# Feed-forward of a fused two-layer network on one core: 704 hidden units in six tiles of 128 rows instead of eight of 88, and 28 TensorE products without a reader

## The reference, cut to what matters

```python
def _act_fake_quant(x, clip_factor):
    scale = jax.nn.sigmoid(clip_factor) * jnp.max(jnp.abs(x)) / QMAX
    return jnp.clip(_ste_round(x / scale), -QMAX - 1.0, QMAX) * scale
...
xq = _act_fake_quant(x, clip_x[0])                                      # x: (16, 113, 256)
gate = jnp.einsum('bsh,ih->bsi', xq, _weight_fake_quant(w_gate))        # i = 704 units
up = jnp.einsum('bsh,ih->bsi', xq, _weight_fake_quant(w_up))
h = _act_fake_quant(jax.nn.silu(gate) * up, clip_down[0])
return jnp.einsum('bsi,hi->bsh', h, _weight_fake_quant(w_down))
```

## Time and profile before

| | |
|---|---|
| median of 3 runs | 865.48 us (865.08 to 865.71) |
| the profiled execution | 865.44 us, of which the span of its instructions 863.5 us |
| PE busy over the span | 699.7 us (81%) |
| DVE, ACT, POOL busy | 520.7, 392.2, 351.2 us |
| mean granted clock of TensorE | 0.89 of full speed |
| end of the state-space stage, start of the feed-forward | about 776 us |
| first and last start of a gate or up product (L1620) | 791.7, 819.8 us |
| first and last start of a down product (L1634) | 832.0, 859.1 us |

### The profile page before, as it was taken

How to read it: one execution, slowest core, us unless ns; L and a number is a source line. 1 busy time by engine, 2 the same in 40 slices (tenths; PEclk the granted TensorE clock), 3 DMA queues, 4 the chain that set the end, 5 groups by cost and what they waited for, 6 DMA issues and landing times. The chain is left out here.

```text
span 863.5 us, 12104 instructions
## 1 busy us (share of the span) xinstructions
PE 699.7 (81%) x3696; PEld 474.2 (55%) x3697; DVE 520.7 (60%) x931; ACT 392.2 (45%) x858; POOL 351.2 (41%) x332
## 2 busy tenths in 40 slices
PE   7699999997999957999994788897788785535958
PEld 5577777775655524665663555455456452213557
DVE  1555555555231102544436568988988988974974
ACT  0465555554422103233222456665665662106973
POOL 0021111110035802323221158878878888420625
PEclk9899999997999968999997789999999997566955
DMA  9990000000002153111114202201210220000002
GB/s 274 335 416 20 0 0 0 0 2 0 1 7 39 31 104 114 44 49 43 43 36 98 88 1 87 87 29 59 86 54 34 87 87 0 0 0 1 0 11 76
DMA packets 28696, 52.73 MB, mean 61 GB/s; under 512 B 10965, under 2 KB 23545, under 8 KB 26489
## 3 DMA queue, kind: packets, MB, share of 16 engines
q1 hardware_dynamic: 19929, 47.49, 16.6%
q0 software_dynamic: 8736, 4.85, 2.2%
HBM read 42.62 MB, written 9.60 MB: 60 GB/s over the span
## 5 line engine op out<-in xcount | busy, mean ns | idle before, releaser
L480 POOL TENSOR_TENSOR arena<-arena 128x904 f32<-128x904 f32 x64 | 124.8, 1953 | 59.3 <-DVE arena L1244 53.0
L1244 DVE TENSOR_TENSOR_SCAN arena<-ps,arena 128x452 f32<-128x452 f32 x128 | 133.5, 1085 | 6.7 <-ACT ps L768 2.1
L768 ACT ACTIVATE ps<-arena,sh_w 128x448 f32<-128x448 f32 x128 | 80.3, 635 | 107.7 <-DVE arena L1244 106.9
L1704 PE MATMUL ps<-arena,const 128*128 128x452 f32 x112 | 63.2, 650 | 41.3 <-POOL arena L484 41.3
L554 ACT ACTIVATE work<-ps,work 113x113 f32<-113x113 f32 x256 | 67.1, 420 | 56.3 <-DVE work L899 56.3
L1528 PE MATMUL ps<-arena,work 128*128 x176 | 86.5, 618 | 0.3 <-issue 0.3
L428 POOL TENSOR_TENSOR xT<-work 128x452 f32<-128x452 f32 x16 | 15.1, 943 | 157.7 <-DVE work L888 157.7
L1234 DVE TENSOR_TENSOR arena<-arena,ps 128x904 f32<-128x904 f32 x64 | 69.2, 1082 | 11.1 <-PE ps L1691 10.7
L511 POOL DMA_INDIRECT slots_in<-xn,slot x16 | 37.9, 2366 | 74.1 <-issue 74.1
L484 POOL TENSOR_TENSOR arena<-arena 128x452 f32<-128x452 f32 x56 | 64.1, 1144 | 4.4
L527 POOL DMA_INDIRECT answers_e<-work,slot_token x22 | 23.7, 1076 | 101.5 <-DVE work L1033 101.5
(11 more groups left out here) (239 smaller groups left out, 1428.5 us busy)
## 6 DMA issues: line engine op xcount, KB each, us to landing
arena<-c_rows SPq DMA_DIRECT2D x8, 1808.0 KB, 6.5
arena<-in_ex_w SPq DMA_DIRECT2D x8, 1536.0 KB, 23.6
slots_in<-work SPq DMA_DIRECT2D x1, 2827.0 KB, 22.3
work<-slots_in SPq DMA_DIRECT2D x22, 128.5 KB, 2.1
xn<-answers_e SPq DMA_DIRECT2D x4, 448.0 KB
out<-resid SPq DMA_DIRECT2D x8, 224.0 KB
arena<-in_patches SPq DMA_DIRECT2D x3, 576.0 KB, 6.0
sh_w<-in_sh_w SPq DMA_DIRECT2D x1, 1536.0 KB, 11.4
```

What stands on the lines that cost most here:

```text
L480: pool.tensor_tensor(read[kp], state[kp], c_all[par][:, 2 * c:2 * c + 2, :].unsqueeze(2).broadcast_to([P, 2, KT, N]), ALU.mult)\
L768: act.activation(decay_ps(n)[:, :, 1:], delta[par].rearrange("p k (b s) -> p (k b) s", b=GB)[:, :, 1:], ACT.Exp, scale=a_neg[:, 2 * c + n: ...
L1244: dve.tensor_tensor_scan(state[kp][:, n].rearrange("p k s -> p (k s)"), decay_ps(n).rearrange("p q s -> p (q s)"), drive[kp][:, n].rearran ...
L1704: pe.matmul(ps[:, 6, 0:KT * N], ident, read[kp][:, 0].rearrange("p k s -> p (k s)"), start=False, stop=False, skip_group_check=True).then_ ...
```

## The change

`FT, FP` becomes 6, 128: five full tiles and one of 64 real units. For the weights of gate and up the last tile is filled by repeating unit 703, so `hid` has 64 rows of copies in it, which don't change a maximum; the down projection uses only the first 64 rows of the last tile (`FLAST`). All operations over a tile now have 128 partitions, the rounding of a piece has 6 x 226 elements per partition instead of 8 x 226. The weight tiles in the expert stage go from 16 to 12, and the four steps that no longer carry one are written out. Gate and up are no longer in loops on any engine: 24 tiles are written out one after the other, with the same order of work. And `keep_busy` on TensorE makes products of 452 columns into a bank that nobody reads again: 12 as soon as VectorE's last product is done, 4 behind the spread of the scale, 12 ahead of the down projection.

```diff
-FFN, FT, FP = 704, 8, 88
+FFN, FT, FP = 704, 6, 128
+FLAST = FFN - (FT - 1) * FP
...
         def pe_ffn(pe):
+            def keep_busy(products):
+                for _ in range(products):
+                    pe.matmul(ps[:, 4, 0:4 * S], identb[:, :], xqT[:, 0, 0:4 * S], start=True, stop=True)
+
...
-            with pe.Fori(0, FG) as g:
-                for m in range(FT):
-                    pair = m % 4
-
-                    pe.wait_ge((hid_even, fup_ready)[m % 2], g * (FT // 2) + m // 2 + 1)
...
+            for i in range(FG * FT):
+                g, m, pair = i // FT, i % FT, i % 4
+
+                pe.wait_ge((hid_even, fup_ready)[i % 2], i // 2 + 1)
...
+            pe.wait_ge(fgate_ready, FG * FT)
+            pe.wait_ge(hid_even, FG * FT // 2 + 2)
+            keep_busy(12)
             scales(1, FP)
+            keep_busy(4)
 
             pe.wait_ge(dscale_ready, KT)
             for k in range(KT):
                 last = pe.matmul(ps[:, 6, k * P:(k + 1) * P], onesf[:, :], diag_d[:, k, :], start=True, stop=True, skip_group_check=True)
             last.then_inc(dscaleT_ps, 1)
+            keep_busy(12)
             for b in range(B):
...
                 for m in range(FT):
-                    last = pe.matmul(ps[0:S, b % 4, 0:D], hq[:, m, b * S:(b + 1) * S], dq[:, m, :], start=m == 0, stop=m == FT - 1)
+                    rows = slice(0, FP if m < FT - 1 else FLAST)
+                    last = pe.matmul(ps[0:S, b % 4, 0:D], hq[rows, m, b * S:(b + 1) * S], dq[rows, m, :], start=m == 0, stop=m == FT - 1)
...
-            for n in range(4):
+            for n in range(FT // 2):
                 act.wait_ge(wqT_ps, 2 * FT + n + 1)
-                act.activation(dq[:, 2 * n:2 * n + 2, :], ps[0:FP, 1 + n, :].rearrange("p (m d) -> p m d", m=2), ACT.Copy).then_inc(wqT_ready, 1)
+                for m in range(2 * n, 2 * n + 2):
+                    rows = slice(0, FP if m < FT - 1 else FLAST)
+                    last = act.activation(dq[rows, m, :], ps[rows, 1 + n, m % 2 * D:(m % 2 + 1) * D], ACT.Copy)
+                last.then_inc(wqT_ready, 1)
...
-            with act.Fori(0, FG // 2) as turn:
-                for m2 in range(2 * FT):
...
+            for i in range(FG * FT):
+                m, pair = i % FT, i % 4
...
-            with dve.Fori(0, FG - 1) as g:
-                products_and_maxima(g)
-            products_and_maxima(FG - 1, last=True)
+            for i in range(0, FG * FT, 2):
+                if i + 4 < FG * FT:
+                    product(i + 4)
+                greatest(i)
+                greatest(i + 1)
```

More of the change, by code:

```diff
@@ L181, in build @@
         sh_w = sb("sh_w", [P, EW])
-        xn2_named = sb("xn2", [S, B, D + 1])
+        xn2_all = sb("xn2", [P, B, D + 1])
+        xn2_named = xn2_all[0:S]
         xn2 = xn2_named[:, :, 0:D]
@@ L218, in build @@
         e_y = [pl.take((D,)) for _ in range(2)]
-        w_int = [pl.take((D // 2,), 88).bitcast(BF16) for _ in range(2)]
+        w_int = [pl.take((D // 2,), FP).bitcast(BF16) for _ in range(2)]
         slot_token = sb("slot_token", [P, ETILES], I32)
@@ L445, in pool_ffn @@
             pool.sem_inc(hid_odd, 2)
[L446 to L450, removed]
+            for i in range(1, FG * FT, 2):
+                g, m = i // FT, i % FT
+                pool.wait_ge(fgate_ready, i + 1)
+                pool.wait_ge(fup_ready, i // 2 + 3)
+                pool.tensor_tensor(hid[:, m, g * 4 * S:(g + 1) * 4 * S], f_up[i // 2 % 2], f_gate[i % 4], ALU.mult).then_inc(hid_odd, 1)
             for b in range(B):
@@ L646, in act_experts @@
                     step(2 * i + par, par, True)
+            for j in range(4 + 2 * FT, ETILES - 2):
+                step(j, j % 2, False)
             gate(ETILES - 1, 1)
@@ L1131, in dve_ffn, with product, greatest @@
             dve.sem_inc(hid_even, 2)
[L1133 to L1142, removed]
[L1143 to L1159 removed]
+            def product(i):
+                g, m = i // FT, i % FT
+                dve.wait_ge(fgate_ready, i + 1)
+                dve.wait_ge(fup_ps, i + 1)
+                dve.scalar_tensor_tensor(out=hid[:, m, g * 4 * S:(g + 1) * 4 * S], in0=ps[0:FP, 2 * (i % 4) + 1, 0:4 * S],
+                                         scalar=uscale[:, m:m + 1], in1=f_gate[i % 4], op0=ALU.mult, op1=ALU.mult).then_inc(hid_even, 1)
+            def greatest(i):
+                g, m = i // FT, i % FT
+                dve.wait_ge((hid_even, hid_odd)[i % 2], i // 2 + 3)
+                dve.tensor_reduce(fmax[:, i:i + 1], hid[:, m, g * 4 * S:(g + 1) * 4 * S], AX.X, ALU.max,
+                                  apply_absolute_value=True).then_inc(hmax_ready, 1)
+            product(0)
+            product(2)
+            for i in range(0, FG * FT, 2):
[3 more added lines that the diff above has]
+                greatest(i + 1)
             dve.wait_ge(hmax_ready, FG * FT)
@@ L1572, in pe_experts @@
                     step(2 * i + par, par, 16 * i + 32, True)
-            assert 4 + 2 * FT == ETILES - 2
+            for j in range(4 + 2 * FT, ETILES - 2):
+                step(j, j % 2, 8 * (j - j % 2) + 32, False)
             down(ETILES - 2, gate_up(ETILES - 1, 1, ETILES - 2))
@@ L1588, in pe_weights_down @@
             pe.wait_ge(eh_ready, ETILES)
-            for n in range(4):
+            for n in range(FT // 2):
                 for m in range(2 * n, 2 * n + 2):
+                    rows = FP if m < FT - 1 else FLAST
                     for k in range(KT):
                         at = m % 2 * D + k * P
-                        last = pe.transpose(ps[0:FP, 1 + n, at:at + P], raw_d[:, k, m * FP:(m + 1) * FP], ident)
+                        last = pe.transpose(ps[0:rows, 1 + n, at:at + P], raw_d[:, k, m * FP:m * FP + rows], ident)
                 last.then_inc(wqT_ps, 1)
         def pe_ffn(pe):
+            def keep_busy(products):
+                for _ in range(products):
+                    pe.matmul(ps[:, 4, 0:4 * S], identb[:, :], xqT[:, 0, 0:4 * S], start=True, stop=True)
             def scales(turn, parts):
```

45 lines of the change are left out of this document (19 added, 26 removed).

## The result

The changed kernel takes 845.2 us (median of 4, 843.9 to 848.0) and the kernel before, timed beside it, 865.6: a ratio of 0.9754, interval 0.9736 to 0.9772. The forecast was 848.8 with a range from 846.3 to 851.6: right in sign and nearly in size, but 1.1 us too slow at its lower end. The profiled execution after took 846.07 us, 19.4 less than the 865.44 of the one before; the prediction's sum was 16.6.

The account below looks back on a forecast made before the run. TensorE bounds the experts and down projection, nearly all engines but GpSimd gate and up. Gains of 7.5 + 0 + 0 + 9.1 = 16.6 us from 865.4 give 848.8 us, range 846.3 to 851.6.

Parts of the forecast that it names:

- I take 0: Expert stage: fewer transposes and larger weight loads would net 0, between 1.0 us gained and 0.4 lost.
- Gate and up: Start of the feed-forward: fewer tile pairs and one table load less would gain 7.5 us.
- The table load: ScalarE while gate and up are formed: code without a loop loads its table once, gaining 0.9 us.
- the four pairs: Tile pairs of gate and up go from 16 to 12, at 1.659 us each: 6.6 us gained.
- The chain: Small steps forming the scale before the down projection: taken as 0, between 0.6 us gained and 0.4 lost.
- The down projection: Last feed-forward part: TensorE at 2.4 GHz no longer the bound, VectorE pacing at 5.55 us per two turns; 9.1 us gained.
- TensorE's twelve products 1.3: Tail of the down projection, behind ScalarE's last rounding: twelve products at 2.4 GHz would take 1.3 us.
- (a): Rival: down projection stays at 1.2 GHz, TensorE bound for 20.6 us; 850.7 to 853.1 us in all; chance 0.14.
- (b): Rival: less GpSimd disturbance of VectorE and a warm scale chain; 845.5 us at the utmost, likelier about 847; chance 0.16.
- (c): Rival: written-out code for gate and up is not there in time, kernel slower than before; chance 0.02.
- (d): Rival: fuller rows, not the products nobody reads, keep the clock; under 1 us, inside the forecast, no chance of its own.

Follow-up runs that it names:

- its own run: Kernel before with only ScalarE's two-pass loop over the gate and up weights written out: 866.08 us, ratio 0.9991.
- full rows: Changed kernel with the down projection's sixth product over all 128 rows (lower weights zero): 842.76 us; also without the 28 products that nobody reads: 844.96 us.

## Why the prediction was right and where it failed

**The failed step** is in the expert stage: "some 64 rows of 1 KB more come in with each, in time before the first tile is wanted", and with it "I take 0". It asked when the weights themselves are wanted and not who stands behind them on the same queue, and it counted rows and bytes where the rate was what changed. The third tile's slots stood behind them, TensorE waited 5.74 us for these, and the trace of before showed that wait with its releaser. Measured in place of 0: 4.15 us in the profiled pair, 3.74 of it up to the third turn (18.26 to 14.52 us behind T0); the other 0.4 is not assigned. The kernel before with 96-row loads has this gain with nothing else changed, and splitting the changed kernel's loads takes it away. That the row count of the two loads is the cause is shown; how much of it is the transfer's rate and how much SyncE's slower issuing stays open.

**Gate and up: right.** 7.84 us against 7.5: the last product moved from 45.28 to 37.44 us behind the statistics. The table load is 0.83 of it by its own run, the four pairs 7.0 (forecast 6.6).

**The chain: right.** 8.64 to 8.44 us from the last product to clip 0: 0.2 gained, inside 0.6 gained to 0.4 lost. The first twelve products, 2.47 us, are hidden; the clock fell once and came back during the last twelve (3.65 us for them), as forecast.

**The down projection: mechanism right, mis-sized.** Clip 0 to the last answer fell from 30.3 to 22.64 us, 7.7 gained instead of 9.1. The pace of VectorE's turns was right (5.48 against 5.55), and the last clip was 0.7 early. The term that was wrong is "TensorE's twelve products 1.3" in the tail: the clock had fallen, each set of six took 1.64 us, so the last piece's two took 3.3 and began 0.4 late behind the piece before; the tail is 2.1 us longer. At 1.00 too twelve take 1.9, and 1.5 with full rows. The reason given for a warm stage, five of six products over 128 rows, doesn't bear it: without the products that nobody reads it is cold for all its 26 us.

**The rivals.** (a), a cold down projection, came only for its last 7 us, but it is what the 64-row product brings as soon as the products that nobody reads are gone; its "one in six" was the right thing to fear, and its price of 20.6 us, from 0.215 a product, was too low: 26.25. (b) had too little disturbance in it, and there was as much as forecast. (c): in gate and up the only idle time put down to issue is that of the weight loads while the clock is at 0.50, 0.22 us a load, and before it was 0.18. (d), the products that nobody reads are worth nothing, is false for this kernel (6.5 us) and true with full rows (0.4).

**The range** took in the down projection's doubt and gave the experts 1.0 at most. 848.8 less 4.15 there, 0.3 in gate and up and 0.2 in the chain, and with 1.4 more in the down projection and 0.6 in the two stages that the sum left alone, is 846.1, the profiled execution, just below the range; the median is 0.9 lower still. Had the down projection come out as forecast, the miss would have been 1.4 us larger: that the time is so near the range is in part luck.

## What to carry to other kernels

When the row count of a transfer changes, ask what is queued behind it and what the transfer's rate will be, and not only when its own data are wanted: in the same twelve us of the stage the core's DMAs moved 188 GB/s with 88 rows in two of the loads, 259 with 96 and 308 with 128, and the wait that shrank was another load's. Look at the issuing queue too, which took 12.86 us for the same instructions before and 10.26 after. A wait that is removed may uncover one on another engine that had been hidden under it (ScalarE's 8.5 us here), and it can cost more than its length, since TensorE's clock may fall in it (1.7 us of slower products behind a wait of 2.1). One short product in a group of six decided whether 28 filler products were worth 6.5 us or 0.4: zero the missing rows and run it full.

## What the runs showed of the hardware that was not expected

- TensorE's granted clock went with the rows of the products and not only with how busy it was. It held 1.00 at 9.30 us busy of 15 with every product over 128 rows; it fell at 3.81 of 5 with every sixth over 64, and at 5.55 of 8 with all over 88. From 0.50 it rose about 3 us behind the stage's first product with all over 128, and not in 26 us without a gap with every sixth over 64, nor in the old stage over 88. The Trainium skill (TensorE: Matmul & The Clock Gate, What's actually happening) has activity release the throttle; these runs show that a TensorE full of products over few rows is not enough.
- Twelve products of which every sixth sums over 64 rows take 1.90 us at 1.00, twelve over 128 take 1.50; 24 with such sixths take 6.59 at 0.50, 0.27 each, where the old stage took 0.215 a product over equal rows. Equal rows cure it: the 64-row product costs some 0.2 us a group at 1.00. The weight loads stand idle for 0.18 us ahead of each 64-row one, so my reading is that the load at a change of the row count is not hidden beside the running product; a 64-row product that is slow by itself was not told apart from that.
- Two loads of 88 rows and two of 40 in place of two of 128 cost 7.5 us of kernel time, with the same bytes to the same place and two more instructions to issue.
